# Perceiver layer on one core: a head's softmax sums shared between TensorE, GpSimd and accumulating DMA transfers

## The reference, cut to what matters

```
q = (x @ Wq + bq)   # 16 heads of 32
k = (y @ Wk + bk)   # 8192 keys
v = (y @ Wv + bv)
scores = einsum('bnhd,bmhd->bhnm', q, k) * scale
attn = softmax(scores, axis=-1)
out = einsum('bhnm,bmhd->bnhd', attn, v)
```

## Time and profile before

| | us |
|---|---|
| median of 3 runs | 1385.35 |
| the three runs | 1385.23, 1385.35, 2734.39 |
| span of the profiled execution | 1383.2 |
| busy in the span: TensorE matmul / VectorE / ScalarE / GpSimd | 1332.2 / 1120.9 / 806.1 / 778.7 |

### The profile page before, as it was taken

The page is one execution under the profiler, slowest core; times in us unless marked ns, Lnnn a source line. Parts: engine busy times, 40 slices in busy tenths (PEclk is TensorE's granted clock), DMA queues, the critical chain, the costliest instruction groups (busy, mean ns, idle before and its releaser), DMA issues. The chain is left out here.

```text
span 1383.2 us, 39979 instructions
## 1 busy us (share of the span) xinstructions
PE 1332.2 (96%) x17098; PEld 702.8 (51%) x17098; DVE 1120.9 (81%) x1786; ACT 806.1 (58%) x1459; POOL 778.7 (56%) x320
## 2 busy tenths in 40 slices
PE   7999999998999999999999999999999999999898
PEld 4444444443555555555555555545555445566454
DVE  5778888887888888888888888888887746578895
ACT  4454444443777777776777776776777841354332
POOL 0322222122899988988998898899889100201121
PEclk9999999999999999999999999999999999999999
DMA  8568777786352122122212112211210030491000
GB/s 265 177 169 231 207 211 211 210 238 177 91 183 69 39 69 67 30 65 67 69 39 68 56 38 69 67 50 57 59 66 31 5 145 1 92 214 41 0 9 23
DMA packets 127799, 137.54 MB, mean 99 GB/s; under 512 B 44995, under 2 KB 108995, under 8 KB 125699
## 3 DMA queue, kind: packets, MB, share of 16 engines
q1 hardware_dynamic: 127622, 134.98, 34.6%
HBM read 75.70 MB, written 44.17 MB: 87 GB/s over the span
## 5 line engine op out<-in xcount | busy, mean ns | idle before, releaser
L1297 DVE TENSOR_REDUCE early<-attend_banks 128x1 f32<-128x512 f32 x952 | 612.4, 685 | 80.8 <-PE attend_banks L1042 75.6
L1261 ACT ACTIVATE attend_prob<-attend_banks 128x512 f32<-128x512 f32 x1024 | 536.0, 599 | 200.8 <-PE attend_banks L1079 198.6
L1439 POOL TENSOR_TENSOR early<-early,attend_prob 128x1024 f32<-128x1024 f32 x210 | 614.5, 2926 | 37.7 <-ACT attend_prob L1261 9.6
L1079 PE MATMUL attend_banks<-early,k_first 97*32 97x512 f16 x2560 | 258.9, 382 | 3.1 <-ACT attend_prob L1261 3.1
L1042 PE MATMUL attend_banks<-k_first,early 96*32 96x512 f16 x2272 | 235.1, 382 | 1.1 <-PEq L285 1.1
L1079 PE MATMUL attend_banks<-early,attend_k_rest 97*32 97x512 f16 x1536 | 154.1, 381 | 2.8 <-ACT attend_prob L1261 2.8
L1042 PE MATMUL attend_banks<-attend_k_rest,early 96*32 96x512 f16 x1536 | 155.8, 380 | 0.0
L1103 PE MATMUL attend_banks<-attend_prob,ones 128*32 128x128 f32 x3048 | 134.3, 272 | 3.6 <-DVE attend_recip L1309 3.6
L1092 PE MATMUL attend_banks<-attend_prob,wkv_area 128*32 128x512 f32 x1024 | 134.1, 592 | 0.0
L1092 PE MATMUL attend_banks<-attend_prob,attend_vh_odd 128*32 128x512 f32 x1024 | 133.6, 592 | 0.0
L503 POOL TENSOR_TENSOR project_w_whole<-project_grid,project_qscale 128x704 f32<-128x704 f32 x24 | 33.3, 1386 | 173.0 <-DVE project_grid L636 173.0
(11 more groups left out here) (220 smaller groups left out, 1823.6 us busy)
## 6 DMA issues: line engine op xcount, KB each, us to landing
v_scratch<-project_v SPq DMA_DIRECT2D x16, 1024.0 KB, 8.9
early<-in_ctx_dram SPq DMA_DIRECT2D x16, 768.0 KB, 6.2
k_first<-k_scratch SPq DMA_DIRECT2D x36, 256.0 KB, 3.5
k_scratch<-project_k_hi SPq DMA_DIRECT2D x64, 128.0 KB, 2.9
k_scratch<-project_k_lo SPq DMA_DIRECT2D x64, 128.0 KB, 3.1
attend_vh_odd<-v_scratch SPq DMA_DIRECT2D x8, 1024.0 KB, 5.0
wkv_area<-v_scratch SPq DMA_DIRECT2D x7, 1024.0 KB, 4.8
attend_k_rest<-k_scratch SPq DMA_DIRECT2D x24, 256.0 KB, 3.5
```

What stands on the lines that cost most here:

```text
L1079: last = nc.tensor.matmul(s_ps[c * HD:(c + 1) * HD, s_bank[n], :], key_rows[:, c * HD:(c + 1) * HD], q_stack[0:KROWS + 1, h, :], start=Tru ...
L1261: nc.scalar.activation(prob[:, q % PSLOTS, t, :], s_ps[:, s_bank[BT * q + t]], ACT.Exp, scale=SCALE).then_inc(p_ready, 1)
L1297: nc.vector.tensor_reduce(part_max[:, s, j, part:part + 1], pre_ps[:, bank], AX.X, ALU.max).then_inc(pre_read, 1)
L1439: nc.gpsimd.tensor_tensor(sums, sums, prob[:, q % PSLOTS, 0:n], ALU.add).then_inc(pool_summed, 1)
```

## The change

For heads 0 to 14, in the even quads from 2 to 14 (seven quads of a head) `pool_tiles` falls from 2 to 1, and the other three tiles of the quad are summed by a DMA that GpSimd issues: the first (quad 2) copies them into `sum_dma`, a new buffer of three tiles for each parity of the head, and the six others add to it (`accum_op`). Each is 128 partitions x 1536 float32, 768 KB, from SBUF to SBUF. In these quads TensorE has no tile left in `add_to_denominator`. The odd quads and quads 0 and 1 stay as they were: 3 tiles by GpSimd, one by TensorE. So a head has 21 tiles by transfers, 34 by GpSimd's additions and 9 by TensorE. `denominator` sums three tiles more (`sum_dma`) and waits for the seventh transfer.

GpSimd's queue gets seven issues a head, each behind that quad's addition. An issue (`send`) waits until all four exponentials of the quad are done and until the transfer before has landed. ScalarE, before it writes a quad of the ring, also waits until the transfer out of the quad four back has landed. The last head is unchanged.

```
--- before.py
+++ after.py
+DMA_TILES = 3
...
             sum_pool = piece([2, POOL_TILES * T])
+            sum_dma = piece([2, DMA_TILES * T])
...
             def pool_tiles(q):
-                return POOL_TILES if q < 2 or q % 2 else POOL_TILES - 1
+                return POOL_TILES if q < 2 or q % 2 else 1
+
+            def dma_tiles(q):
+                return DMA_TILES if q >= 2 and q % 2 == 0 else 0
...
+            def dma_upto(h, q):
+                return sum(dma_tiles(p) > 0 for p in range(QUADS)) * h + sum(dma_tiles(p) > 0 for p in range(q + 1))
+
+            def den_upto(h, q):
+                of_head = [summed_tiles(h, p) < BT for p in range(q + 1)]
+                return sum(summed_tiles(0, p) < BT for p in range(QUADS)) * h + sum(of_head)
...
             def summed_tiles(h, q):
-                if not (isinstance(h, int) and h == H - 1):
-                    return pool_tiles(q)
+                if not last_head(h):
+                    return pool_tiles(q) + dma_tiles(q)
                 return DVE_TILES if q < LAST_SUMMED else 0
...
 add_to_denominator:
+                    if summed_tiles(h, q) == BT:
+                        return
...
 denominator:
                         pe.wait_ge(pool_summed, QUADS * (h + 1))
+                        pe.wait_ge(dma_summed, 16 * dma_upto(h, QUADS - 1))
                         tiles = POOL_TILES
+                        for n in range(DMA_TILES):
+                            for t in range(TT):
+                                nc.tensor.matmul(den_ps[t * HD:(t + 1) * HD, 0:P], ones[:],
+                                                 sum_dma[:, s, n * T + t * P:n * T + (t + 1) * P],
+                                                 start=False, stop=False)
...
 scalar head:
-                        wait(act, den_added, Q + 1 - PSLOTS)
+                        if Q >= PSLOTS:
+                            wait(act, den_added, den_upto(*divmod(Q - PSLOTS, QUADS)))
                         if last > 0 or q < PSLOTS:
                             wait(act, pool_summed, Q + 1 - PSLOTS)
+                            if Q >= PSLOTS:
+                                wait(act, dma_summed, 16 * dma_upto(*divmod(Q - PSLOTS, QUADS)))
...
 gpsimd:
+                def send(i, s, q):
+                    h, n = 2 * i + s, pool_tiles(q)
+                    if not dma_tiles(q):
+                        return
+                    pool.wait_ge(p_ready, BT * (quad_no(i, s, q) + 1))
+                    target = sum_dma[:, s]
+                    source = prob[:, q % PSLOTS, n:n + DMA_TILES].rearrange("p n t -> p (n t)")
+                    wait(pool, dma_summed, 16 * (dma_upto(h, q) - 1))
+                    if q == 2:
+                        wait(pool, den_ready, h - 1)
+                        pool.dma_start(target, source).then_inc(dma_summed, 16)
+                    else:
+                        pool.dma_start(target, source, accum_op=ALU.add).then_inc(dma_summed, 16)
+
+                for h in range(H - 1):
                     for q in range(QUADS):
+                        add_up(*divmod(h, 2), q)
+                        send(*divmod(h, 2), q)
```

More of the change, by code:

```diff
@@ L881, in perceiver @@
             pool_summed = sem("pool_summed")
+            dma_summed = sem("dma_summed")
             pv_read = sem("pv_read")
@@ L931, in pool_tiles, with last_head @@
             def pool_tiles(q):
-                return POOL_TILES if q < 2 or q % 2 else POOL_TILES - 1
+                return POOL_TILES if q < 2 or q % 2 else 1
+            def dma_tiles(q):
+                return DMA_TILES if q >= 2 and q % 2 == 0 else 0
+            def last_head(h):
+                return h == H - 1
+            def dma_upto(h, q):
[3 more added lines that the diff above has]
+                return sum(summed_tiles(0, p) < BT for p in range(QUADS)) * h + sum(of_head)
             LAST_SUMMED = QUADS - 2
             def summed_tiles(h, q):
-                if not (isinstance(h, int) and h == H - 1):
-                    return pool_tiles(q)
+                if not last_head(h):
+                    return pool_tiles(q) + dma_tiles(q)
                 return DVE_TILES if q < LAST_SUMMED else 0
@@ L1440, in add_up @@
                                                 ALU.add).then_inc(pool_summed, 1)
-                for s in range(2):
-                    for q in range(QUADS):
[L1444 to L1450, removed]
+                def send(i, s, q):
[12 more added lines that the diff above has]
+                for h in range(H - 1):
+                    for q in range(QUADS):
+                        add_up(*divmod(h, 2), q)
+                        send(*divmod(h, 2), q)
         xattn.close()
```

## The result

The changed kernel takes 1498.99 us, the median of 4 runs (1490.14 to 1503.58), against 1385.29 us: a ratio of 1.081 with a 95% interval of 1.078 to 1.084. That is 114 us slower. One of the four runs of the kernel before took 2734.39 us, nothing on record says why, and the ratio leaves it out. The forecast of 1352.4 us was wrong in sign, and the time lies above the range, which ended at 1460. Rival A, the transfers as the bound, was the right mechanism, and even its 1454 us were 45 too few.

What follows compares the result with a forecast made beforehand. TensorE's queue was taken as the bound: a span of 1383.2 - 36 (TensorE's tiles) + 3 (VectorE) = 1350.2 us, with the median 2.15 above it, gave 1352.4 us. Own range 1347 to 1358; whole range 1347 to 1460.

Steps and rivals of the forecast that it cites:

- Rival A: Transfers become the bound: accumulations move their bytes twice and `send` serialises them; 69 us more, 1454 us; chance 0.28.
- TensorE is the bound, and 11 tiles a head go: TensorE's queue sets the pace; 11 tiles net at 0.22 us save 2.4 us a head, 36 us in 15 heads.
- VectorE: Reductions keep up with shorter quads; catching up after the reciprocal costs 0.2 us a head, 3 us; at worst 25 us.
- GpSimd: Additions of 36.7 us plus seven issues at 1 us make 43.7 us a head, which fits into 46.4.
- Rival C: GpSimd's issues become the bound: at 2 us an issue, 28 us more, 1414 us; chance 0.10.
- The transfers: the step that failed: Seven serial transfers a head, each taking 5.7 us to the next possible issue, stay just short of stalling the kernel.
- C: Time from one transfer's issue to the next possible one, landing included; taken as 5.7 us.
- The two mechanisms I had put at its ends: A 768 KB transfer's price from loads: bytes moved once 4.3 us, or an accumulation's bytes counted twice 6.4 us.
- The traffic beside it: SyncE's own loads, about 2.5 MB a head, fall in part on the chain of transfers: 0.4 us a transfer.
- the 6.0 of the prediction: Limit in us for C in a head's chain: nothing stalls if 4.5 + 7C < 46.4.
- 7C + 3.7: Head's period in us once `denominator` waits for transfers; reaches the old 48.8 at C = 6.44 us.
- The ring's own condition: A ring slot is rewritten three quads, some 8.2 us, later; said to need the same C to within 0.1 us.

Runs made afterwards that it cites:

- e_copy: The changed kernel with all seven transfers of a head as plain copies, without the additions into `sum_dma`: 1372.1 us, ratio 0.989.
- e_free: The changed kernel with transfers between idle buffers; ScalarE and the denominator don't wait for them, GpSimd still waits for each landing: 1507.7 us, ratio 1.087.
- v_two: The changed kernel with two tiles (512 KB) to a transfer instead of three, the third summed by TensorE: 1384.3 us, ratio 0.999.

## Why the prediction was wrong, step by step

**TensorE is the bound, and 11 tiles a head go.** Right in kind: e_copy runs at TensorE's new pace. The size was off: I wrote "11 x 0.22 = 2.4 us a head" and 1.85 was measured in e_copy, since in each of seven quads the removed tile had hidden 0.09 us of waiting for ScalarE.

**VectorE.** 0.2 us a head was allowed and its worst case of 25 us kept as a rival; the waits show 1.2 us in 500, and 0.6 in e_copy, where TensorE sets the pace again. No loss.

**GpSimd.** "I take 1 us" for an issue; it is 0.88, and 0.6 for a copy. One tile at 1.28 was right. Rival C needed an issue of 1.73 us and is refuted by that 0.88.

**The transfers: the step that failed.** "I take the middle of 4.3 and 6.4, 5.3, and 0.4: C = 5.7 us". This term of the sum was mis-sized. C was 7.2 us on average, and the 1.5 us between have three parts:

- The accumulation alone, "5.3". The shortest landings are 5.6 us, and 18 of the 90 accumulations stay below 5.8. That the middle came so near is luck. The two mechanisms I had put at its ends are each 0.8 us shorter than I had them: a copy lands in 3.5 us, not 4.3, and an accumulation in 5.6, not 6.4. I had taken both from loads, whose fixed part (2.25 us) and slope (0.69 us per 256 KB) are both larger than a copy's (1.7 and 0.6).
- The traffic beside it, "0.4". The mean landing is 6.7 us, so the disturbance is 1.1. The loads of keys are a part of it: the 22 accumulations issued within about 1 us of one land in 7.8 us on average, the other 68 in 6.4. The rest is open.
- The step from a landing to the next issue. I priced C by rows that end at the landing and put nothing behind it. It is 0.5 us.

Undisturbed, C would have been 6.1 us, just past the 6.0 of the prediction and below the 6.44 at which the old period is reached. The traffic beside it carried it past that point, to 7.2.

The shortest landings also bear on the two mechanisms. Copies of 512 and 768 KB land in 2.9 and 3.5 us, accumulations in 4.4 and 5.6: 0.6 us for another 256 KB in a copy and 1.2 in an accumulation, twice as much to the tenth that the view shows, on a fixed part of 1.7 and 2.0 us.

The Trainium skill's rule that I had set against my sum (*Collectives: The Full Stack*, "The bandwidth ceiling", two source reads halve the rate) is stated there for the reduce step of a collective. This trace agrees with it in the ratio: 1.2 against 0.6 us per 256 KB. That the second read is the cause, and not the add, no run here shows. I had written the rule down and given it less weight than a midpoint.

**The period from C.** In the head whose issues are shown the six spacings average (724.92 - 681.81) / 6 = 7.2 us; "7C + 3.7" then gives 54.1 us, and from copy to copy it was 736.44 - 681.81 = 54.6. The arithmetic of rival A held. It priced C at 7.1, so a head at 53.4 where 55.7 was the mean, and left out the first head's loss, hence 1454 instead of 1499. The upper end of the range had a slip in its arithmetic: C = 7.2 gives 15 x 5.3 = 80 us, so 1465 and not 1460. The measured time lies above both.

**Who holds whom.** The text had ScalarE's ring and the denominator held by the transfers. e_free shows that this is not needed: with both waits gone the time stays, since the wait before the issue stops GpSimd's additions, which stand behind it in the same queue, and these hold everyone. The ring's own condition was also a little tighter than "the same C to within 0.1 us": by the same rows the sixth transfer lands in time if 0.82 + 5 (C - 5.44) + C < 8.27, so C < 5.8 us. At 7.2 us both are passed.

## What to carry to other kernels

A wait put into the queue of an engine that has other work is paid by all of that work: before adding one, compare the period of the thing waited for (here 7.2 us) with the period at which the queue must turn (5.44 us), and let the wait be on the transfer two back where a second buffer is to be had. That period is more than the transfer's shortest time: it holds the traffic beside it (1.1 us here) and the step from the landing to the next issue (0.5 us). Where two mechanisms give two prices for an unknown operation, the middle is neither; when a threshold lies between them, both sides deserve a fair chance. And filler work between two dependent steps hides their latency: taking it out returns less than its own duration (two tiles of 0.22 us gave 0.35, from 3.05 to 2.70 us).

## What the runs showed of the hardware that I had not expected

- An accumulating transfer within SBUF has twice the slope of a copy (1.2 against 0.6 us per 256 KB, by the shortest landings of v_two and the changed kernel), and its issue on GpSimd takes 0.88 us against 0.57 in e_copy.
- Between the landing of a transfer and the issue that waited for it GpSimd lets 0.5 us pass, 0.8 at most, in all 75 cases of the changed kernel.
- An accumulation that starts beside a load of keys (384 KB) can take 9 us instead of 5.6; beside a load of 2048 KB and one of keys, 9.8 us even for 512 KB (v_two).
- The loads suffer too: the values' 1024 KB landed in 7.7 us (median) in the changed kernel, against 5.0 before.
- TensorE's granted clock went from full to half, that is from 2.4 to 1.2 GHz, after TensorE had stood waiting, for some 72 us in all. Two adjoining windows of the changed kernel (TensorE's busy time in 3 us, its records, the granted clock, DMA share and GB/s):

```profile
606.00:609.00 3.00, 0.86 (x16) 0.89 0.03 6
609.00:612.00 3.00, 3.00 (x31) 0.54 0.82 167
```

  It worked for 0.86 of the first 3 us and stood 2.14 us waiting for an exponential; the mean of the next 3 is 0.54, so almost all of them are at half clock. Filling one gap a head moved the mean clock from 0.976 to 0.982 and not the time.
